# Two graph attention layers on one core: two tiles to a step in 26 of the 32 turns

## What is computed

```python
# layer 0, masked by the adjacency
scores = einsum('bhqd,bhkd->bhqk', q, k) / sqrt(32) + beta * adj_e
scores = where(adj_e > 0, scores, -9e15)
x = layernorm(x + merge_heads(softmax(scores) @ v))
# layer 1, the adjacency as a bias, and an output projection
a = einsum('bnhd,bmhd->bhnm', q, k) * 384 ** -0.5 + adj[:, None]
a = softmax(where(all(a == 0, -1)[..., None], -inf, a)); a = nan_to_num(a)
x = layernorm(x + merge_heads(a @ v) @ Wo.T + bo)
```

## Time and profile before

| | |
|---|---|
| median of three runs | 1065.62 us (1065.01 to 1066.3) |
| profiled execution | 1065.69 us, span 1063.9 us |
| granted TensorE clock, mean | 0.993 of full |
| TensorE matmuls | 1037.8 us busy, 16916 records |
| weight loads (beside the matmuls) | 900.5 us |
| VectorE, GpSimd, ScalarE | 793.6, 789.0, 449.7 us |
| transfers | 53.33 MB, 50 GB/s over the span |

### The profile page before, as it was taken

How to read it: one execution, slowest core, us unless ns; L and a number is a source line. 1 busy time by engine, 2 the same in 40 slices (tenths; PEclk the granted TensorE clock), 3 DMA queues, 4 the chain that set the end, 5 groups by cost and what they waited for, 6 DMA issues and landing times.

```text
span 1063.9 us, 38532 instructions
## 1 busy us (share of the span) xinstructions
PE 1037.8 (98%) x16916; PEld 900.5 (85%) x16916; DVE 793.6 (75%) x1578; ACT 449.7 (42%) x717; POOL 789.0 (74%) x646
## 2 busy tenths in 40 slices
PE   8999999999999999999999999999999999999975
PEld 7887888888888888888888888888888888888874
DVE  4687877868778687786868778687786868877884
ACT  4554434444343443444444344443434434334431
POOL 2688877777787786777778777777877867776775
PEclk9999999999999999999999999999999999999997
DMA  6521112112111121111112011121111210010100
GB/s 189 159 71 52 46 36 63 40 44 62 44 39 47 37 62 44 40 46 50 56 44 62 29 54 39 44 62 44 40 46 37 67 44 5 17 37 10 35 32 31
DMA packets 61750, 53.33 MB, mean 50 GB/s; under 512 B 35984, under 2 KB 55440, under 8 KB 61584
## 3 DMA queue, kind: packets, MB, share of 16 engines
q1 hardware_dynamic: 60752, 49.69, 15.9%
q10 hardware_dynamic: 832, 1.18, 0.3%
HBM read 38.28 MB, written 12.58 MB: 48 GB/s over the span
## 4 chain that ended last, share of the span: by engine, by line
PE 89%; DVE 4%; POOL 3%; issue 2%; DMA 1%; ACT 1%; POOLq 0%; DVEq 0%
PE ps_u L375 53%; PE ps_h L375 9%; PE ps_s L395 8%; PE ps_s L481 8%; PE ps_h L503 7%; PE ps_h L413 2%; PE ps_h L515 2%; DMA xt_in<-in_x_t 1%; POOL probs L827 1%; DVE row_sum L737 1%; DVE probs L696 1%; ACT probs L618 1%; DVE row_max L705 1%; POOL xt_lo L853 1%; POOL probs L833 0%
## 5 line engine op out<-in xcount | busy, mean ns | idle before, releaser
L827 POOL TENSOR_TENSOR probs<-probs,row_max 128x768 f32<-128x768 f32 x128 | 193.1, 1509 | 220.1 <-DVE row_max L705 220.1
L833 POOL TENSOR_TENSOR probs<-probs,row_inv 128x768 f32<-128x768 f32 x128 | 192.9, 1507 | 2.4 <-DVE row_inv L741 2.2
L737 DVE TENSOR_REDUCE row_sum<-probs 128x12 f32<-128x768 f32 x128 | 121.9, 953 | 68.6 <-ACT probs L618 68.6
L580 ACT COPY probs_t<-ps_s 128x768 f32<-128x768 f32 x128 | 102.6, 802 | 109.9 <-PE ps_s L481 109.8
L375 PE MATMUL ps_u<-w_hi_v,xt_lo 128*128 128x384 f32 x384 | 137.8, 359 | 0.0
L375 PE MATMUL ps_u<-w_hi_v,xt_hi 128*128 128x384 f32 x384 | 129.6, 338 | 0.0
L375 PE MATMUL ps_u<-w_lo_v,xt_hi 128*128 128x384 f32 x384 | 129.6, 337 | 0.0
L705 DVE TENSOR_REDUCE row_max<-probs 128x12 f32<-128x768 f32 x128 | 121.3, 948 | 2.2
L618 ACT ACTIVATE probs<-probs 128x768 f32<-128x768 f32 x128 | 108.7, 849 | 28.2 <-POOL probs L827 26.7
L375 PE MATMUL ps_u<-xt_hi,w_lo_q 128*128 128x512 f32 x282 | 120.0, 425 | 0.6 <-ACT q_sb L606 0.6
L375 PE MATMUL ps_u<-xt_hi,w_lo_k 128*128 128x512 f32 x288 | 117.9, 409 | 1.5 <-ACT k_sb L608 0.9
(11 more groups left out here) (82 smaller groups left out, 2106.9 us busy)
## 6 DMA issues: line engine op xcount, KB each, us to landing
x_in<-in_x SPq DMA_DIRECT2D x16, 768.0 KB, 4.5
out<-z SPq DMA_DIRECT2D x64, 192.0 KB, 1.9
xt_in<-in_x_t SPq DMA_DIRECT2D x15, 768.0 KB, 4.8
adj<-in_adj SPq DMA_DIRECT2D x64, 128.0 KB, 3.0
xt_in<-in_x_t SPq DMA_DIRECT2D x3, 256.0 KB, 4.6
q_sb<-in_wq ACTq DMA_DIRECT2D x3, 192.0 KB, 4.8
k_sb<-in_wk ACTq DMA_DIRECT2D x1, 576.0 KB, 6.9
v_sb<-in_wv SPq DMA_DIRECT2D x1, 576.0 KB, 7.1
```

What stands on the lines that cost most here:

```text
L580: nc.scalar.copy(probs_t[:].rearrange("p (a i) n -> p a (i n)", a=2), ps_s[:, 0:2, 0:KT * P]).then_inc(probs_t_ready, 1)
L737: nc.vector.reduce_sum(row_sum[p][:], probs[p][:].rearrange("p i b k -> p (i b) k"), AX_X)\
L827: nc.gpsimd.tensor_tensor(s, s, over_keys(row_max[p]), ALU.subtract).then_inc(shifted, 1)
L833: nc.gpsimd.tensor_tensor(s, s, over_keys(row_inv[p]), ALU.mult).then_inc(probs_ready, 1)
```

## The change

From turn 2 to 27 a turn has two steps of two tiles each (`slots`: tiles 0 and 1, then 2 and 3) in place of four steps; the other turns keep one tile to a step. `cur`, `prev`, `last` and `turned` are now tuples of tiles. A packed step of TensorE makes the scores of both tiles, the early unit, both results, the columns of both turned tiles, both turnings of probabilities, the late units but one, the heads of both tiles, and then that last unit (`behind_heads`), before the next step's scores. The second tile has its scores, turned probabilities, heads and result in places of its own: `ps_s` columns 192 to 383 of each bank, banks 2 and 3 for turned probabilities, `ps_h` columns 192 to 383 of both banks, bank 1 for the result. The turned columns of the input go to `ps_u` as units of kind `"x"`, so the unit two places later waits for their `xt_lo`. `o_hi`, `o_lo` and `o_t` are copied for both tiles in one instruction.

For room `probs` and the row columns get four buffers, `probs_t` two, `o_t`, `o_hi`, `o_lo` double width; `w_stage` goes, and `w_o` is staged where the two `adj1` buffers lie, for which the first load of `adj1` now waits. VectorE, GpSimd and ScalarE take the two tiles of a step in a new order, and SyncE issues a step's stores behind its loads. The core of the diff:

```diff
+def slots(phase):
+
+    if 2 <= phase <= N_TURNS - 5:
+        return [(0, 1), (2, 3)]
+    return [(0,), (1,), (2,), (3,)] if phase < N_TURNS else [(0,), (1,)]
...
+def columns(s):
+
+    return [(*tile[:2], "x", tile[2]) for tile in s.turned if tile[0] == 1]
...
+def behind_heads(s):
+
+    return late(s)[-1:] if len(s.ts) == 2 else []
+
+
+def ahead_of_heads(s):
+    return late(s)[:-1] if len(s.ts) == 2 else late(s)
+
+
+UNIT_ORDER = [u for s in STEPS for u in early(s) + columns(s) + late(s)]
...
             def load_adj1(c):
+                if c == 0:
+                    sp.wait_ge(w_lo_ready, w_count["o1"])
...
+            def bank_free(no):
                 if no > 2:
                     freed = UNIT_ORDER[no - 3]
+                    if freed[2] == "x":
+                        pe.wait_ge(xt_lo_ready[1], low_no((*freed[:2], freed[3])))
+                        return
...
             for s in STEPS:
-                if s.cur:
-                    scores(s.cur)
+                for j, tile in enumerate(s.cur):
+                    scores(tile, j, s)
                 for unit in early(s):
                     if UNIT_NO[unit] > 2:
                         make_unit(unit)
-                if s.last:
-                    result(s.last)
-                if s.turned:
-                    turn_activations(s.turned, s.last)
-                if s.prev:
-                    turn_probs(s.prev, s.cur)
-                for unit in late(s):
+                for j, tile in enumerate(s.last):
+                    result(tile, j, s)
+                for unit in columns(s):
+                    turn_activations(unit)
+                for j, tile in enumerate(s.prev):
+                    turn_probs(tile, j, s)
+                for unit in ahead_of_heads(s):
                     if UNIT_NO[unit] > 2:
                         make_unit(unit)
-                if s.prev:
-                    heads(s.prev, s.turned)
+                for j, tile in enumerate(s.prev):
+                    heads(tile, j, s)
+                for unit in behind_heads(s):
+                    make_unit(unit)
```

The heads wait for the residual of the last tile of the pair before them:

```diff
-                if at(tile) > 0:
-                    pe.wait_ge(z_ready, at(tile))
-                if turned and turned[0] == 1:
-                    pe.wait_ge(xt_lo_ready[1], low_no(turned))
+                if s.last:
+                    pe.wait_ge(z_ready, at(s.last[-1]) + 1)
```

VectorE's step, and GpSimd's:

```diff
-                if s.cur:
-                    bias_and_max(s.cur)
+                for j, tile in enumerate(s.cur):
+                    add_bias(tile, j, s)
+                for tile in s.cur[:1]:
+                    maxima(tile)
...
                 for unit in early(s):
                     unit_out(unit)
-                if s.last:
-                    residual(s.last)
-                if s.turned and s.phase >= 0:
-                    activations_lo(s.turned)
-                if s.cur:
-                    sums(s.cur)
-                for unit in late(s):
+                if s.phase >= 0:
+                    for tile in s.turned:
+                        activations_lo(tile)
+                for tile in s.cur[1:]:
+                    maxima(tile)
+                for j in range(2):
+                    if len(s.ts) == 2:
+                        for unit in ahead_of_heads(s)[j:j + 1]:
+                            unit_out(unit)
+                    for tile in s.last[j:j + 1]:
+                        residual(tile, j)
+                for tile in s.cur[:1]:
+                    sums(tile)
+                for unit in ahead_of_heads(s)[2 if len(s.ts) == 2 else 0:]:
                     unit_out(unit)
+                for tile in s.cur[1:]:
+                    sums(tile)
...
                 if s.prev:
                     heads_lo(s.prev)
+                for unit in behind_heads(s):
+                    unit_out(unit)
...
+                for tile in s.cur[1:]:
+                    shift(tile)
+                for tile in s.last[:1]:
+                    inverse_deviation(tile)
+                    normalise(tile)
+                for tile in s.cur:
+                    scale(tile)
+                for tile in s.last[1:]:
+                    inverse_deviation(tile)
+                    normalise(tile)
```

More of the change, by code:

```diff
@@ L37 @@
 FIRST_AT = [[0, 1], [2, 3], [4, 5], []]
-Step = namedtuple("Step", "phase t cur prev last done turned units")
+Step = namedtuple("Step", "phase ts cur prev last turned units")
 def at(tile):
@@ L377, in split_product, with scores @@
                 return last
-            def scores(tile):
+            def scores(tile, j, s):
                 layer, c, t = tile
@@ L383, in scores @@
                     pe.wait_ge(qk_ready, last_qk((layer, c)))
-                if at(tile) > 0:
+                if j == 0 and at(tile) > 0:
                     pe.wait_ge(biased, at(tile))
-                if at(tile) > 1:
-                    pe.wait_ge(probs_t_ready, at(tile) - 1)
+                if j == 0 and s.last:
+                    pe.wait_ge(probs_t_ready, at(s.last[-1]) + 1)
                 for g in range(KT):
@@ L427, in make_unit, with turn_activations @@
                         pe.wait_ge(qk_ready, QK_NO[freed])
+            def turn_activations(unit):
+                layer, c, _, t = unit
+                no = UNIT_NO[unit]
+                pe.wait_ge(normed, at((0, c, t)) + 1)
+                bank_free(no)
+                for g in range(KT):
+                    last = nc.tensor.transpose(ps_u[:, (no - 1) % 2, g * P:(g + 1) * P],
+                                               x1[c % 3][:, t, g * P:(g + 1) * P], ident[:])
+                last.then_inc(unit_made, 1)
+            def make_unit(unit):
+                layer, c, kind, n = unit
+                p, no = home((layer, c)), UNIT_NO[unit]
+                bank_free(no)
                 w = f"{kind}{layer}"
@@ L519, in result @@
                     last = split_product(
-                        ps_h[:, 0, 0:D], lambda g: o_hi[:, g, :], lambda g: o_lo[:, g, :],
+                        ps_h[:, j, 0:D], lambda g: o_hi[:, j * KT + g, :], lambda g: o_lo[:, j * KT + g, :],
                         lambda g: w_hi["o1"][:, g, :], lambda g: w_lo["o1"][:, g, :])
@@ L568, in activations_hi @@
                 else:
-                    act.wait_ge(xt_made, second_no(tile))
-                    src = ps_h[:, 1, 0:D].rearrange("p (g n) -> p g n", g=KT)
+                    act.wait_ge(unit_made, UNIT_NO[layer, c, "x", t])
+                    src = ps_u[:, (UNIT_NO[layer, c, "x", t] - 1) % 2, 0:D].rearrange("p (g n) -> p g n", g=KT)
                 user = last_user((layer, c))
@@ L713, in activations_lo @@
                 cols = slice(t * P, (t + 1) * P)
-                nc.vector.tensor_tensor(xt_lo[p][:, :, cols], ps_h[:, 1, 0:D].rearrange("p (g n) -> p g n", g=KT),
+                src = ps_u[:, (UNIT_NO[layer, c, "x", t] - 1) % 2, 0:D].rearrange("p (g n) -> p g n", g=KT)
+                nc.vector.tensor_tensor(xt_lo[p][:, :, cols], src,
                                         xt_hi[p][:, :, cols].bitcast(F32), ALU.subtract).then_inc(xt_lo_ready[1], 1)
@@ L733, in sums @@
             def sums(tile):
-                layer, c, t = tile
-                p = t % 2
+                layer, c, p = tile
                 dve.wait_ge(exp_ready, at(tile) + 1)
@@ L784, in _ @@
             for s in STEPS:
-                place = (s.phase, s.t)
+                place = (s.phase, s.ts[0])
                 if place == (-1, 0):
@@ L838, in add_bo @@
                     return
-                pool.wait_ge(xt_made, second_no(tile))
+                pool.wait_ge(unit_made, UNIT_NO[layer, c, "x", t])
                 if second_no(tile) == 1:
```

245 lines of the change are left out of this document (120 added, 125 removed).

## The result

The changed kernel takes **1073.01 us** (median of 5 runs, 1070.33 to 1074.07), the kernel before beside it 1065.62 (1064.85 to 1067.11). The ratio is 1.0063, with a 95% interval of 1.0051 to 1.0075: slower by 7.4 us, where 7.6 us less was forecast. Its profiled execution took 1074.07 us, its span is 1072.3.

A forecast was written before the change was run, and what follows sets the result against it. TensorE, busy 98% of the span and throughout turns 2 to 27, was taken as the bound. Terms -5.2 - 1.0 - 2.5 + 1.0 = -7.7 against 1065.69 gave 1058 us, range 1048 to 1070.

The forecast's parts named there:

- The step that failed: Turns 2 to 27: TensorE never idles today, so only its stream's pace can change or a new wait appear.
- Heads and scores: Small matmuls of two packed tiles: the pair costs 3.02 us instead of 3.12, over 52 steps -5.2 us (ends -12.0 and +10.4).
- The low end of the bounds: Second tile's heads and scores cost what the first's do without the edge: pair 2.89 us, 0.23 less than 3.12.
- The pace after the first 33 records: Within a heads block: 33 of 48 start by 0.27 us, the other 15 take 0.24, 0.016 each.
- the high end: Second tile's heads and scores all go at 0.016 us a record: pair 3.32 us, 0.20 more than before.
- Transposes: TensorE's transposes, six together instead of three: an edge saved is worth 0.01 to 0.03 us, in all -1.0 us.
- The late probabilities: TensorE's 13 waits for GpSimd's probabilities ahead of their turning go, since packed steps give GpSimd time: -2.5 us.
- The level B halves: Tiles 2 and 3: VectorE's z and TensorE reach the heads together, at 10.9 us with layer 1; 0.04 each allowed, +1.0 us.
- the walk: Both halves of a turn followed by VectorE's paces; tiles 2 and 3 come out level, z at 10.9 us with layer 1.
- At nothing: Wider `o_hi` and `o_lo` copies, z's store behind the loads on SyncE, and `w_o` staged in `adj1`: no cost.
- Rival 1: Only edges cost, the second tile's heads and scores go like the first's: gain 12.0 + 1.0 + 2.5 - 1.0 = 14.5, 1051 us; chance 0.27.
- Rival 2: Small matmuls starved: pace falls to 0.016 us after about 33 records, pair costs 0.20 more, +7.9, 1074 us; chance 0.10.

The follow-up runs named there:

- experiment 6: Changed kernel with two units behind the heads, VectorE's residuals ahead of the v units and GpSimd's first normalisation ahead of the second shift: 1055.09 us, ratio 0.99.
- experiment 8: Changed kernel with two units behind the heads, earlier z, and a packed step's loads held until its scores are made: 1049.78 us, ratio 0.9844 to the kernel before.
- Experiment 2: Changed kernel with two units instead of one between heads and next scores, other engines' order kept: 1099.54 us, ratio 1.032 to the kernel before.
- experiment 5: Changed kernel with one tile to a step in all turns, its buffers, engine order and `w_o` staging kept: 1065.07 us, ratio 0.9995 to the kernel before.

## Why the prediction was wrong

- **The step that failed** is the sentence "in the packed turns only the pace of TensorE's own stream can change, or a wait can appear that is not there today", as I then used it: I walked the waits for semaphores and left out the supply of instructions. The stop is such a wait, but no row of before could show it, since single steps do not have it, and no term of the sum stood for it. It costs about 26 us in the profile after, the lower clock behind three of the stops included. The rates that would have raised the question were there: the page of before counts the same 134 transfers for 33832 records of TensorE, one in 8 us, and the order ahead of the forecast shows 402 instructions in a stretch that I had costed at less than 5 us.
- **Heads and scores**: forecast -5.2 us. The mechanism (fewer edges) was right, the size too small. The low end of the bounds, a second tile at what the first costs without its edge, held: 1.17 and 1.21 where 1.18 and 1.29 was that end. The balance asks for 18.0 less 2.5 for the late probabilities, and 2.7 more that the heads' waits for z took back (below): over 52 steps 0.35 each, above my low end of 0.23 and near the 0.34 of the place shown above. The pace after the first 33 records, on which the high end stood, does not rule a block.
- **Transposes**: forecast -1.0 us, no gain at this place, and 0.08 us more. Three and six took 0.33 + 0.57 and an edge of 0.09, twice 1.98; six and twelve take 529.88 to 531.85 and an edge of 0.09, 2.06:

```profile
529.88 0.90 PE L444 MATMUL ps_u<-ident,x 128*128 128x128 f32 x6
530.62 1.47 PE L505 MATMUL ps_s<-ident,probs 128*128 128x128 f32 x12
531.85 0.42 PE L398 MATMUL ps_u<-w_hi_v,xt_lo 128*128 128x384 f32 x1
532.11 0.33 PE L398 MATMUL ps_u<-w_lo_v,xt_hi 128*128 128x384 f32 x1
```

- **The late probabilities**: forecast -2.5 us, and of the 13 waits one of 0.3 us is left.
- **The level B halves**: the walk was right, the price too small: forecast +1.0 us, found 3.2. One second z ends at 536.54 + 0.55 = 537.09 where the heads start at 537.19, 11.3 us after the scores' start where 10.9 was walked, and costs 0.46 us. In the other 25 turns, too, the heads start 0.10 after z has ended:

```profile
536.54 0.55 DVE L811 TENSOR_TENSOR z<-ps_h,x_in 128x384 f32<-128x384 f32 x1
...
571.22 0.55 DVE L811 TENSOR_TENSOR z<-ps_h,x 128x384 f32<-128x384 f32 x1
```
```profile
571.49 0.34 PE L398 MATMUL ps_u<-w_hi_v,xt_hi 128*128 128x384 f32 x1
571.87 1.23 PE L525 MATMUL ps_h<-probs_t,v_sb 64*32 64x64 f32 x96
```

  That is 0.38 from the last unit matmul to the heads, where 0.27 is the edge without a wait (and all 26 such places of experiment 6): 0.11 late, 25 times. The list of waits does not show gaps so short. In experiments 6 and 8, with z earlier, this is gone too. Experiment 2 shows how near a larger loss was.
- **At nothing**: right for the stores and the staging of `w_o` (experiment 5); the wider copies, which experiment 5 does not have, show no wait of their own in the packed turns. The order of loads on SyncE was costed only by whether the data come in time; that they delay another queue was not thought of.
- **The rivals.** Rival 1 had the right gain from packing (14.5 us forecast, 18 found; experiment 8, with the stops and the waits for z nearly gone, is 15.6 us faster than the kernel before beside it). Rival 2 gave the right time, 1074, for the wrong reason: there is no slower pace after 33 records, there are whole stops at a few places, while most blocks of 96 run through in 1.21 us. Its word, starved, was near; what was short was the list, not a queue filled during a unit.

## What to carry to other kernels

Before small instructions are packed together, count how many the engine issues per microsecond, and compare with the rate at which its queue of instructions fills. Here a block was some 252 records, and TensorE went on 2.2 to 2.9 us after the block's transfer had begun. A stretch of more than a block (here 402 instructions in 4.6 us) can stop where a border in it is reached sooner than that, and stops longer if large loads issued just ahead make the transfer start late. Such a stop shows as idle time without a releaser (or with one that had long ended) in the middle of a block without waits; its place, counted in records, is a whole number of blocks from the next stop, and it moves against the program when instructions are added far ahead. The remedies here were a thinner stretch (a second long unit in it) and loads issued behind it; and a unit put behind a consumer takes from the time that other engines had ahead of it, so their order has to follow.

## What was not expected of the hardware

- Transfers of data delay the transfers of instructions: the stops inside the scores fall from 13.8 to 3.2 us when the loads shrink, with nothing else changed, and the same block's transfer starts with 169 records left in place of one.
- A stop can have an aftermath. After 2.4 us without a matmul the granted clock was at 0.50 from 475.7 to 479.1, and nine 512-column matmuls took 3.48 us from 476.27 on in place of 2.18, 1.3 us on top of the stop. The same came behind the stops at 115.56 (2.29 us long) and 279.03 (2.04), but not behind that at 668.84 (2.47): there the clock stayed at 1.00 and the nine took 2.18. What parts them was not tried.
- In a block of 96 small records the mean distance from start to start is 1.21 / 96 = 0.013 us, with two records to a product.
- The trace does not show when a block is asked for, so how the loads hold its transfer back (a shared queue, shared engines or the memory) stays open. Why the scores stop and the heads hardly ever do was not tried apart, though they are the second dense portion in 4.6 us.
